# Storing the odd maps of a convolution net twice, one column apart, so that TensorE reads 512 columns in one run

## The reference, cut to what matters

```python
def basic_block(x, w1, w2, stride=1, ds=None):
    out = relu(conv3(x, w1, stride) * BN_S)
    out = conv3(out, w2, 1) * BN_S
    identity = conv1x1(x, ds, stride) * BN_S if ds is not None else x
    return relu(out + identity)

x0 = gn(x)
x = basic_block(x0, e0b0c1, e0b0c2)                              # level 0, 64x64
x = basic_block(x, e0b1c1, e0b1c2); f0 = x
x = basic_block(x, e1b0c1, e1b0c2, stride=2, ds=e1b0ds)          # level 1, 32x32
x = basic_block(x, e1b1c1, e1b1c2); f1 = x
x = basic_block(x, e2b0c1, e2b0c2, stride=2, ds=e2b0ds)          # level 2, 16x16
x = basic_block(x, e2b1c1, e2b1c2)
x = (relu(deconv2(x, dec0w) * BN_S) + f1) * BN_S
x = (relu(deconv2(x, dec1w) * BN_S) + f0) * BN_S
out = x_in + x
```

## Time and profile before

| what | value |
|---|---|
| median of 3 runs | 91.69 us (91.61 to 91.88) |
| the profiled execution, its own time | 91.54 us |
| its span in the trace | 89.7 us |
| mean granted TensorE clock over the span | 0.98 of full |
| TensorE busy, weight loads busy | 92%, 82% of the span |
| DVE, ACT, POOL busy | 71%, 50%, 31% of the span |

### The profile page before, as it was taken

One profiled execution on the slowest core, in us unless ns is written; L12 is line 12 of the kernel. 1 busy time (PEld: TensorE's weight loads), 2 busy tenths in 40 slices (PEclk: granted clock), 3 DMA queues, 4 the chain that ended last, 5 costly groups with the idle time before them and its releaser, 6 DMA issues.

```text
span 89.7 us, 1547 instructions
## 1 busy us (share of the span) xinstructions
PE 83.0 (92%) x537; PEld 73.9 (82%) x537; DVE 63.7 (71%) x189; ACT 44.9 (50%) x94; POOL 27.5 (31%) x43
## 2 busy tenths in 40 slices
PE   5988999999999999999999999999999989999900
PEld 3666999998777799999977777999999989887600
DVE  5579999799968799655635569999638797543650
ACT  6007015877435065744423259999910089990410
POOL 7300070999910000654440000300794002400140
PEclk9999999999999999999999999999999999999975
DMA  2989900045673003550000000000000000000075
GB/s 23 255 251 324 323 22 0 7 122 125 154 217 112 4 14 121 168 168 5 0 0 0 0 0 4 0 0 0 7 0 0 4 0 0 7 0 0 0 258 210
DMA packets 4183, 6.51 MB, mean 73 GB/s; under 512 B 464, under 2 KB 2128, under 8 KB 4176
## 3 DMA queue, kind: packets, MB, share of 16 engines
q1 hardware_dynamic: 4032, 6.29, 23.0%
q10 hardware_dynamic: 144, 0.13, 0.4%
HBM read 5.37 MB, written 1.05 MB: 72 GB/s over the span
## 4 chain that ended last, share of the span: by engine, by line
PE 83%; DVE 7%; DMA 3%; issue 1%; ACT 1%; POOLq 1%; DVEq 0%
PE psum L837 78%; DMA x_sb<-x_in 3%; PE psum L876 2%; DVE stats L611 2%; DVE split L727 1%; PE psum L972 1%; POOLq L167 1%; DVE shared L682 1%; PE psum L1029 1%; DVE split L734 1%; PE psum L862 1%; DVE moments L626 1%; DVE shared L640 1%; PE psum L869 1%; ACT result L586 0%
## 5 line engine op out<-in xcount | busy, mean ns | idle before, releaser
L470 POOL TENSOR_TENSOR odd<-relu,odd 128x363 fp32r<-128x363 f32 x12 | 13.4, 1134 | 16.0 <-ACT odd L545 16.0
L837 PE MATMUL psum<-shared,w_e0b0c 128*128 128x364 f32 x72 | 12.5, 332 | 0.4 <-DVE shared L640 0.4
L837 PEld LDWEIGHTS psum<-shared,w_e0b0c 128*128 128x128 f32 x72 | 12.0, 189 | 0.7 <-issue 0.7
L837 PE MATMUL psum<-shared,w_e0b1c 128*128 128x364 f32 x72 | 12.2, 329 | 0.0
L837 PEld LDWEIGHTS psum<-shared,w_e0b1c 128*128 128x128 f32 x72 | 12.1, 188 | 0.1
L837 PE MATMUL psum<-odd,w_e0b1c 128*128 128x512 f32 x48 | 12.0, 411 | 0.0
L837 PE MATMUL psum<-odd,w_e0b0c 128*128 128x512 f32 x48 | 12.0, 411 | 0.0
L763 DVE SCALAR_TENSOR_TENSOR relu<-psum,inside 128x363 f32<-128x363 f32 (+2 forms) x18 | 8.7, 489 | 3.8 <-PE psum L837 3.6
L837 PEld LDWEIGHTS psum<-odd,w_e0b0c 128*128 128x128 f32 x48 | 9.1, 190 | 2.6
L837 PEld LDWEIGHTS psum<-odd,w_e0b1c 128*128 128x128 f32 x48 | 9.1, 190 | 2.6
L545 ACT ACTIVATE odd<-relu 128x363 fp32r<-128x363 f32 x12 | 6.2, 520 | 7.4 <-DVE relu L763 7.4
(11 more groups left out here) (126 smaller groups left out, 140.4 us busy)
## 6 DMA issues: line engine op xcount, KB each, us to landing
x_sb<-x_in SPq DMA_DIRECT2D x4, 160.0 KB, 3.9
raw<-e0b0c_in SPq DMA_DIRECT2D x2, 256.0 KB, 4.7
raw<-e0b1c_in SPq DMA_DIRECT2D x2, 256.0 KB, 4.9
raw<-e1b1c_in SPq DMA_DIRECT2D x2, 256.0 KB, 3.2
raw<-e2b1c_in SPq DMA_DIRECT2D x2, 256.0 KB, 2.6
raw<-e1b0c_in SPq DMA_DIRECT2D x1, 448.0 KB, 3.6
raw<-e2b0c_in SPq DMA_DIRECT2D x1, 448.0 KB, 4.1
x_sb<-x_in SPq DMA_DIRECT2D x2, 192.0 KB, 3.9
```

Of the source, the lines that this page charges most:

```text
L470: pool.tensor_tensor(split_of(piece, 1), fp32_of(piece), split_of(piece, 0).bitcast(F32), ALU.subtract).then_inc(lo_ready, 1)
L837: last = pe.matmul(target, w, moving, start=(first and n == 0), stop=(final and n == len(terms) - 1), skip_group_check=skip)
```

## The change

`odd0` keeps each odd map of level 0 twice in each half: version 0 holds columns 0 to 31 of the 33 rows and version 1 columns 1 to 32, both with rows 32 apart. ACT writes the high part in two activations a piece and POOL the low part in two subtractions, 11 rows of 32 columns each, and a matmul of an even piece takes 16 rows of version sx as one run of 512 columns. The larger `odd0` takes the room of `skip0`, which now lies in the memory of `block0`; so ACT waits for its own scaling of both images (`skip0_scaled`) before it writes the skip. At level 2, e2b0c1 does the products with high and low weights image by image (20 matmuls of 82 columns in place of 10 of 82 and 5 of 164 columns), and ACT puts two of the corner copies of image 0 behind the side copies of image 1.

```diff
--- before.py
+++ after.py
@@ -38,7 +38,6 @@
 ODD_COLS = [b + 1 for b in BLOCKS]
 FLAT_PITCH = BLOCKS[0] + 1
 FLAT = (BLOCKS[0] + 2) * FLAT_PITCH + 2
-ODD0_PITCH = 36
 PITCH = [b + 1 for b in BLOCKS]
 MAP = [(b + 2) * (b + 1) + 2 for b in BLOCKS]
 RUN = [(b + 1) * (b + 1) + 1 for b in BLOCKS]
@@ -175,14 +174,15 @@
         x_sb = sb("x_sb", [P, IMAGES, 32, 32])
         normed = sb("normed", [P, IMAGES, 32, 32])
         block0 = sb("block0", [P, IMAGES, 32, 32])
-        skip0 = sb("skip0", [P, 8, IMAGES, 2, 8, 8])
+        skip0 = block0[:].rearrange("p i r c -> p (i r c)").rearrange("p (n i j a b) -> p n i j a b", n=8, i=IMAGES,
+                                                                     j=2, a=8)
         skip1 = sb("skip1", [P, 2, 2, 2, IMAGES, 8, 8], F32R)
         result = sb("result", [P, 8, IMAGES * 2 * 64])
         split0 = sb("split0", [P, 2, IMAGES, 2, 2, MAP[1]], F32R)
         split1 = sb("split1", [P, 2, IMAGES, 2, 2, MAP[2]], F32R)
         planes = [None, split0, split1]
-        odd0 = sb("odd0", [P, 2, IMAGES, ODD_ROWS[0], ODD0_PITCH], F32R)
-        flat1 = odd0[:].rearrange("p h i r c -> p (h i r c)")[:, 0:2 * IMAGES * MAP[1]].rearrange(
+        odd0 = sb("odd0", [P, 2, IMAGES, 2, ODD_ROWS[0], BLOCKS[0]], F32R)
+        flat1 = odd0[:].rearrange("p h i v r c -> p (h i v r c)")[:, 0:2 * IMAGES * MAP[1]].rearrange(
             "p (h i n) -> p h i n", h=2, i=IMAGES)
         flat2 = sb("flat2", [P, 2, IMAGES, MAP[2]], F32R)
         flat = [None, flat1, flat2[:]]
@@ -197,7 +197,7 @@
         odd1 = shared[:, 2 * odd1_size:3 * odd1_size].rearrange("p (h i n) -> p h i n", h=2, i=IMAGES)
         corner1 = shared[:, 3 * odd1_size:3 * odd1_size + corner1_size].rearrange(
             "p (h i n) -> p h i n", h=2, i=IMAGES)
-        odd = [odd0[:, :, :, :, 0:ODD_COLS[0]], odd1, odd2[:]]
+        odd = [None, odd1, odd2[:]]
         corner = [None, corner1, corner2[:]]
         sides = [None, sides_1, shared[:, 0:4 * IMAGES * RUN[2]].rearrange("p (s h i n) -> p s h i n", s=2, h=2,
                                                                          i=IMAGES)]
@@ -362,8 +362,6 @@
 
             stage = STAGES[piece.stage]
             if stage.level == 0:
-                if stage.kind == "odd":
-                    return odd[0][:, half, piece.images[0], piece.row:piece.row + piece.rows, :]
                 return flat_inside(half, piece.images, piece.row, piece.rows)
             return odd[stage.level][:, half] if stage.level == 2 else odd[1][:, half, piece.images[0]]
 
@@ -379,6 +377,9 @@
 
         def skip0_of(n):
             return skip0[:, n].rearrange("p i j a b -> p (i j a b)")
+
+        def shifted_of(piece, half, shift):
+            return odd0[:, half, piece.images[0], shift, piece.row:piece.row + piece.rows, :]
 
         def side_copy(level, image, copy, run=None):
 
@@ -467,8 +468,11 @@
             for piece in LEVEL0:
                 if STAGES[piece.stage].residual is None:
                     wait_half(pool, piece.index, 0)
-                    pool.tensor_tensor(split_of(piece, 1), fp32_of(piece), split_of(piece, 0).bitcast(F32),
-                                       ALU.subtract).then_inc(lo_ready, 1)
+                    for shift in range(2):
+                        last = pool.tensor_tensor(shifted_of(piece, 1, shift),
+                                                  fp32_of(piece)[:, :, shift:shift + BLOCKS[0]],
+                                                  shifted_of(piece, 0, shift).bitcast(F32), ALU.subtract)
+                    last.then_inc(lo_ready, 1)
 
 
             pool.wait_ge(summed, last_piece(STAGE["e0b1c2"], range(IMAGES), BLOCKS[0] - 1) + 1)
@@ -541,6 +545,11 @@
                         last = act.activation(planes_inside(1, 0, piece.images[0], i, piece.row // 2, piece.rows // 2),
                                               fp32_of(piece)[:, i::2].rearrange("p r (c b) -> p b r c", b=2), ACT.Relu)
                     last.then_inc(hi_ready, 1)
+                elif STAGES[piece.stage].kind == "odd":
+                    for shift in range(2):
+                        last = act.activation(shifted_of(piece, 0, shift),
+                                              fp32_of(piece)[:, :, shift:shift + BLOCKS[0]], ACT.Relu)
+                    last.then_inc(hi_ready, 1)
                 else:
                     act.activation(split_of(piece, 0), fp32_of(piece), ACT.Relu).then_inc(hi_ready, 1)
                 if piece.index + 1 < len(WEIGHTS):
@@ -564,10 +573,13 @@
             gather_corners(1, 1)
             scale_skip0(1)
             gather_sides(2, 0)
-            gather_corners(2, 0)
+            gather_corners(2, 0, range(2))
             gather_sides(2, 1)
+            gather_corners(2, 0, range(2, 4))
             gather_corners(2, 1, range(3, 4))
             for image in range(IMAGES):
+                if image == 0:
+                    act.wait_ge(skip0_scaled, IMAGES)
                 act.wait_ge(skip0_added, image + 1)
                 for q in range(4):
                     for i in range(2):
@@ -906,8 +918,6 @@
                 flat_columns = piece.rows * FLAT_PITCH + piece.rows * FLAT_PITCH % 2
                 if stage.kind == "odd" and level == 0:
                     target = bank_of(piece)[:, 0:flat_columns]
-                elif level == 0:
-                    target = rows_0(target, piece)
 
                 terms = []
                 if stage.shortcut == "identity":
@@ -945,8 +955,8 @@
                         first = (piece.row + sy) * FLAT_PITCH + sx
                         return flat0[:, half, images[0], first:first + flat_columns]
                     if level == 0:
-                        return odd[0][:, half, images[0], piece.row + sy:piece.row + sy + piece.rows,
-                                      sx:sx + BLOCKS[0]]
+                        rows = odd0[:, half, images[0], sx, piece.row + sy:piece.row + sy + piece.rows, :]
+                        return rows.rearrange("p r c -> p (r c)")
                     source, run = (odd, EVEN_RUN) if stage.kind == "even" else (flat, RUN)
                     return of_images(source[level][:, half], level, sy * PITCH[level] + sx, run[level], images)
 
@@ -968,12 +978,12 @@
                     if level == 2:
                         for image in images:
                             wait_half(pe, source_of_level(2, image), 0)
-                            for n, m in enumerate(whole[0]):
-                                pe.matmul(target[:, image], w[:, 0, n], m[:, image], start=(image == 0 and n == 0),
-                                          stop=False, skip_group_check=True)
-                        wait_w_lo(pe, k)
-                        products(target, [(w[:, 1, n], m) for n, m in enumerate(whole[0])], first=False, final=False,
-                                 skip=True)
+                            wait_w_lo(pe, k)
+                            for part in range(2):
+                                for n, m in enumerate(whole[0]):
+                                    pe.matmul(target[:, image], w[:, part, n], m[:, image],
+                                              start=(image == 0 and part == 0 and n == 0),
+                                              stop=False, skip_group_check=True)
                     else:
                         wait_source(piece, 0)
                         wait_w_lo(pe, k)
```

## The result

The changed kernel takes 93.19 us (median of 4 runs, 93.07 to 93.78), the kernel before beside it on the same chip 91.78 (4 runs): 1.0166 times the time before, interval 1.0138 to 1.0194. The forecast was 91.7, no change that can be measured, its range 90.7 to 92.6: the kernel is slower, and outside the range. The profiled execution took 93.2, its span is 91.4.

A forecast was written before the change was run, and what follows sets the result against it. TensorE, busy 92% of the span, was taken to bound the kernel. Stall +0.9, cheaper matmuls -0.8 and level 2 -0.05 gave +0.05 on 91.54; forecast 91.7, no measurable change, range 90.7 to 92.6.

The forecast's parts named there:

- The matmul: Level 0's 96 matmuls of 512 columns: 0.231 us each as one run, 0.015 saved each, up to 1.44 for all.
- B: Level 0 matmuls: a run costs only its streaming, 512 columns about 0.216, result 90.9 to 91.0; chance 0.07.
- C: Level 0 matmuls: only the even start saves, 512 columns cost 0.240, result 92.2; chance 0.13.
- D: Level 0 matmuls: 512 columns stay at 0.246 and the stall is paid whole, 92.5; chance 0.03.
- POOL's turns and the stall: e0b0c2: POOL alternates with DVE, piece 4's low copies come at 29.1, 1.3 late; its group begins 0.9 later than now.
- Rival A: e0b0c2: DVE's turns fall behind POOL's, stall small or absent, 90.3 without any; chance 0.15.
- E: e0b0c2: the 1.3 us stall lowers TensorE's clock, 16 matmuls at 1.2 GHz, +3.1, near 94.8; chance 0.02.
- What is saved after the stall: e0b0c2 and e0b1c2: 52 cheaper matmuls behind the stall save 0.015 each, 0.8 in all; the last 12 give nothing.
- Level 2: e2b0c1: five more matmuls fill TensorE's 0.46 wait for image 1's high part; gain 0 to 0.1, taken as 0.05.
- the forecast's own signs: Distances 0.231, POOL gapless to about 30.8, one 1.3 us wait near 27.8, level 1 near 56.0, wait near 72.8 gone.
- the wait ahead of the sides: Level 1: TensorE waits about 0.2 us before image 1's side products.
- another wait over 0.3 in level 0: Level 0: a further wait of over 0.3 us, besides the one near 28, would show the forecast wrong.

The follow-up runs named there:

- g1: f2 with DVE's border masks of level 1 made behind piece 5 instead of piece 7: 91.94 us, 1.0011 times the kernel before.
- h2: f2 with two idle 256-column matmuls ahead of piece 18 of e0b1c2: 1.0077 times the kernel before.
- h1: f2 with two idle 256-column matmuls ahead of piece 17 of e0b1c2: 1.0096 times the kernel before.
- f2: The changed kernel with 16 one-column POOL memsets added behind its last subtraction: 92.32 us, 1.0054 times the kernel before.
- g4: f2 with four idle 256-column matmuls ahead of piece 19, the last of e0b1c2: 1.0073 times the kernel before.
- f1: The kernel before with 12 one-column POOL memsets added behind its last subtraction: 92.37 us, 1.008 times the kernel before.
- f3: The changed kernel with both copies written by one 704-column instruction, on ACT and on POOL: 93.88 us, 1.0223 times the kernel before.

## Why the prediction was wrong, step by step

**The matmul: right.** 0.2325 for one run of 512 columns against 0.231 forecast; rivals B (0.216), C (0.240) and D (0.246) are out. The rule of the Trainium skill, "TensorE: Matmul & The Clock Gate", section "Back-to-back issue gap", is 0.017 too short at 512 and 0.013 at 364. The section gives it for an isolated matmul, which the prediction left out, and about 131 ns for 512 columns in a stream; no stream here shows that.

**POOL's turns and the stall: right.** Piece 4's low copies end at 29.28, in an execution that starts 0.17 later; 29.1 was forecast. The low group is 0.89 late against 0.9. That the turns make it is shown by g1, where one DVE job out of the way gives 0.87 back. Rival A fell, and so did E: behind the stall the distances are 0.233 again from the second on.

**What is saved after the stall: wrong, the first step that failed.** The text had "4 + 12 matmuls of e0b0c2 and 36 of e0b1c2: 52 x 0.015 = 0.8". Of the 0.89, 0.31 came back (0.58 at the sides). The count goes: 16 matmuls of e0b0c2 by 0.013 = 0.21, less 0.10, since the first distance behind the stall is 0.334 and not 0.233; e0b1c1 0.02; and 24 matmuls of e0b1c2, not 36, by 0.013 = 0.32, less about 0.13: DVE's casts at 56.55 take 1.07 instead of 0.94, beside POOL's memsets, which TensorE's earlier end sets off. That is 0.32, for the 0.8 of the text. The forecast had seen that the last piece gives nothing, from DVE's unbroken work behind it. It hadn't gone back along that chain, past DVE to ACT's gather; h2 shows that piece 18 gives almost nothing either, h1 that piece 17 gives all. The casts' term is no constant: by where the memsets fall the pair takes 0.93 (g1), 0.94 (h2), 1.06 (f2), 1.09 (h1) or 1.20 (g4).

**Level 2: right in size.** 0 to 0.04 for 0.05.

**The tail: missing.** The sum ended at the last product, and everything behind it was taken to stay as it was. The forecast worked out what 12 more POOL instructions cost in time and not that they lengthen a list that is itself loaded by DMA, and a range that held every term of the sum couldn't hold this one. 0.93 here, 0.90 in f1. With it and the 0.5 of the step above, +0.05 becomes about 1.5. The tail alone puts the time outside the range: f2, without it, takes 92.32. Of the forecast's own signs, the stall, the distances and the wait ahead of the sides stood nearly as said. Level 1 starts 0.13 later than before (35.80 against 35.67), where 0.06 earlier was forecast. What it named as proof of error, another wait over 0.3 in level 0, did not come; a distance of 0.36 that it did not foresee stands at 59.04, in level 1.

## What to carry to other kernels

When a saving is followed to the end, go back from where it is to arrive, over every engine of that chain, to the first instruction that hangs on the saved work: in which piece that lies decides how many of the cheaper instructions count. When a helper engine gets more work, ask which instructions of its neighbour it now stands beside, also much later; doubling only the operand that an engine with time to spare writes (ACT's high part) gave 1.0% where doubling both cost 0.5% (f2), and 1.7% with the late packet. And compare the packets of the instruction queues before and after: twelve more on POOL's list moved a load into the final stores, and sixteen idle ones moved it out (30 more on ACT's did nothing).

## What the runs showed of the hardware

- One 8 KB packet of POOL's instruction list, in time with the final stores, makes the span 0.90 to 0.93 longer; 16 idle POOL memsets (0.6 us where POOL has nothing to do) remove it. The packet takes 1.11 to 1.17 us, and the last eight output packets follow it one at a time.
- POOL and DVE take whole turns: with a POOL instruction of 704 columns DVE's 512 take 1.62, with 352 columns 0.7 to 1.2, alone 0.69. The Trainium skill, "SBUF — State Buffer", section "SBUF: two separate sides", calls the port pair an exclusive lock and the loser fully blocked; f3 agrees in kind. The hand-over comes somewhat before an instruction's recorded end, as the earlier trace rows had it.
- A stall of TensorE costs 0.10 beyond its end: the first matmul distance behind it is 0.334 where 0.233 is usual.
- A distance of 1.6 us between two matmul starts in a busy stretch left TensorE at 2.4 GHz in the changed kernel; in the profiled execution of f3, distances of 1.80 and 0.86, 1.6 apart, were followed by 3.4 us at 1.2 GHz, which cost 1.4.
